# A convolution with three raw weight buffers, weight chunks mixed one ahead of their split, and the sums of the second sweep formed in place

## The reference, cut to what matters

```
x = lax.conv_general_dilated(inputs, conv_w, window_strides=(1,), padding='SAME',
                             dimension_numbers=('NWC', 'WIO', 'NWC')) + conv_b     # inputs (2, 2048, 1024), conv_w (3, 1024, 768)
q, k, v = jnp.split(x, 3, axis=-1)
# blocks of 128 tokens, 16 heads of 64: scores, causal softmax, values, two projections
x = _layernorm(x_in + attention_and_projections(q, k, v))
x = _layernorm(x + ffn(x))            # dense layer plus a mixture of low-rank experts
```

## Time and profile before

| | |
|---|---|
| time, median of 3 runs (lowest, highest) | 1656.67 us (1656.15, 1661.89) |
| time of the profiled execution | 1654.62 us |
| its span | 1652.8 us |
| PE busy in the span | 1566.8 us (95%) |
| DVE, ACT busy | 1183.8 us (72%), 610.5 us (37%) |
| matmuls of the convolution | 3456, from 14.4 to 463.1 us |
| first matmul after the convolution | 488.25 us |

### The profile page before, as it was taken

How to read it: one execution, slowest core, us unless ns; L and a number is a source line. 1 busy time by engine, 2 the same in 40 slices (tenths; PEclk the granted TensorE clock), 3 DMA queues, 4 the chain that set the end, 5 groups by cost and what they waited for, 6 DMA issues and landing times. The chain is left out here.

```text
span 1652.8 us, 29301 instructions
## 1 busy us (share of the span) xinstructions
PE 1566.8 (95%) x10816; PEld 1397.9 (85%) x10816; DVE 1183.8 (72%) x2785; ACT 610.5 (37%) x1729; POOL 260.7 (16%) x227
## 2 busy tenths in 40 slices
PE   6998999699938999999999999899999999999998
PEld 6998999699936888888888888689898988989897
DVE  6858857776656666666666667778878877887884
ACT  4223322322225776767667667611111111111110
POOL 0000000000001100101001010433333333333331
PEclk9999999899969999999999999999999999999999
DMA  7886564667850010110101021411121122112111
GB/s 291 329 277 259 211 214 164 210 232 270 292 195 6 2 52 1 51 51 0 51 0 51 28 80 54 143 62 58 62 81 57 57 74 69 57 67 76 57 42 51
DMA packets 55157, 181.05 MB, mean 110 GB/s; under 512 B 5552, under 2 KB 13872, under 8 KB 48432
## 3 DMA queue, kind: packets, MB, share of 16 engines
q1 hardware_dynamic: 53360, 173.81, 30.3%
q10 hardware_dynamic: 1728, 6.29, 1.0%
HBM read 125.49 MB, written 54.53 MB: 109 GB/s over the span
## 5 line engine op out<-in xcount | busy, mean ns | idle before, releaser
L588 PE MATMUL conv_acc<-x_split,weights 128*128 128x256 f32 x3456 | 423.6, 286 | 39.7 <-DVE weights L497 14.6
L588 PEld LDWEIGHTS conv_acc<-x_split,weights 128*128 128x128 f32 x3456 | 421.0, 194 | 42.2 <-issue 20.3
L1522 PE MATMUL ps_f<-weights 128*128 128x266 f32 (+2 forms) x1728 | 329.6, 344 | 0.0
L1522 PEld LDWEIGHTS ps_f<-weights 128*128 128x128 f32 x1728 | 277.5, 189 | 23.8
L1010 DVE CUSTOM_DVE_ANT_0 scores_and_probs<-ps_scores,causal_mask 128x128 f32<-128x128 f32 x512 | 118.6, 287 | 126.1 <-PE ps_scores L1130 122.2
L917 ACT ACTIVATE scores_and_probs<-scores_and_probs,score_neg_max 128x128 f32<-128x128 f32 x512 | 197.9, 392 | 4.8 <-DVE score_neg_max L1015 4.7
L1358 ACT ACTIVATE gate_exp<-h_and_gate,gate_neg_max 128x8 f32<-128x8 f32 x32 | 9.6, 301 | 349.6 <-DVE gate_neg_max L1433 349.6
L1101 PE MATMUL ps_v<-weights 128*128 128x512 f32 x384 | 106.2, 413 | 30.1 <-PEq L134 24.9
L355 ACT ACTIVATE x_split<-x_planes 128x1024 fp32r<-128x1024 f32 x48 | 51.0, 1062 | 210.7 <-PE conv_acc L588 166.6
L1522 PE MATMUL ps_f<-late_weights,weights 128*128 128x266 f32 (+2 forms) x576 | 116.1, 337 | 0.0
L475 DVE TENSOR_TENSOR x_split<-x_planes,x_split 128x1024 fp32r<-128x1024 f32 x48 | 58.7, 1223 | 75.3 <-ACT x_split L355 75.0
(11 more groups left out here) (136 smaller groups left out, 2355.8 us busy)
## 6 DMA issues: line engine op xcount, KB each, us to landing
x_raw<-in_xT SPq DMA_DIRECT2D x32, 1028.0 KB, 6.8
conv_tile<-in_x SPq DMA_DIRECT2D x32, 512.0 KB, 3.8
out<-out_tile SPq DMA_DIRECT2D x32, 512.0 KB, 2.7
conv_tile<-convT_scratch SPq DMA_DIRECT2D x16, 768.0 KB, 6.4
conv_tile<-in_conv_w SPq DMA_DIRECT2D x8, 1152.0 KB, 6.7
weight_stage<-in_conv_w SPq DMA_DIRECT2D x8, 1152.0 KB, 9.0
ce_scratch<-conv_l SPq DMA_DIRECT2D x16, 512.0 KB, 7.8
x_planes<-ce_scratch SPq DMA_DIRECT2D x16, 512.0 KB, 4.4
```

Of the source, the lines that this page charges most:

```text
L588: last = nc.tensor.matmul(acc[f][:, k, :], w[:, c, a, k, f * P:(f + 1) * P], xs[:, j % XS, b, k, c % CPG, :], start=(c == 0 and k == 0 and ...
L1522: mm = nc.tensor.matmul(ps_f[par][n][:, 0:b0 - a0], x1T[:, par, a, kc, :], wf[kc][:, b, a0:b0], start=(kc == 0 and k == 0), stop=(n == 2 a ...
```

## The change

Four things are done, all in `conv_phase`.

1. `conv_y` grows to the size of a raw weight chunk (128 x 2304) and becomes a third buffer for them: the load of chunk n now waits until chunk n - 3 is split, instead of n - 2. SP's loads of weights move: three before each boundary in single iterations, then in the iterations 17 to 20 and 32 to 34 those of chunks 3 and 4, 5 and 6, and 7, each right behind that iteration's load of inputs.
2. DVE mixes one chunk ahead of the split, and all of it stands at the end of the iteration: chunk 0 in iteration 14 (30), then in the iterations 15 to 18 (31 to 34) mix chunk c + 1, split chunk c, for two c. In the iterations from 31 on, the mix of the next inputs stands ahead of the weights, not behind.
3. Evacuation has three buffers, one for each pair p: the two of `conv_m` and `features_out`, which had been unused in the convolution. The first sweep, which had four, has these three as well.
4. `finish_first` writes sum and difference in place of its input, the second from the first, and SP stores from there. ACT therefore waits in the second sweep, and in the first unit of the third, until the stored piece (u - 1, p) has landed (`sd_stored`), no longer until DVE has read it.

The diff, cut to its core:

```diff
-    M_COUNT = 4
+    M_COUNT = FP
+    WR = 3
...
-        wraw = [craw[:, 0:TAPS * KTAPS].rearrange("p (k n) -> p k n", k=TAPS),
-                attn.stages[:, 0:TAPS * KTAPS].rearrange("p (k n) -> p k n", k=TAPS)]
...
-        ybuf = sb("conv_y", [P, 2 * QUAD * UQ], F32)
+        ybuf = sb("conv_y", [P, TAPS * KTAPS], F32)
+        wraw = [a.rearrange("p (k n) -> p k n", k=TAPS)
+                for a in (craw[:, 0:TAPS * KTAPS], attn.stages[:, 0:TAPS * KTAPS], ybuf[:])]
...
-        m = [pair_view(mbuf[:, i, :]) for i in range(2)]
-        y_half = [pair_view(ybuf[:, i * HALF:(i + 1) * HALF]) for i in range(2)]
-        m_first = m + y_half
-        sd = y_half
+        m = [pair_view(mbuf[:, i, :]) for i in range(2)] + [pair_view(attn.out[:].rearrange("p f n -> p (f n)"))]
...
             def load_w(n):
-                if n >= 2:
-                    sp.wait_ge(w_lo, n - 1)
+                if n >= WR:
+                    sp.wait_ge(w_lo, n - WR + 1)
...
-                sp.dma_start(sd_dram[n_of[u], p], sd[e % 2]).then_inc(sd_stored[e % 2], 16)
+                sp.dma_start(sd_dram[n_of[u], p], m[p]).then_inc(sd_stored[p], 16)
...
-                if j == 10:
-                    load_w(CC)
-                    load_w(CC + 1)
-                if 18 <= j < 18 + GRAN - 1:
-                    load_w(CC + CPG * (j - 17))
-                    load_w(CC + CPG * (j - 17) + 1)
-                if j == 26:
-                    load_w(2 * CC)
-                    load_w(2 * CC + 1)
+                if 10 <= j < 10 + WR:
+                    load_w(CC + j - 10)
+                if 17 <= j < 17 + GRAN:
+                    for n in range(CPG * (j - 17) + WR, min(CPG * (j - 16) + WR, CC)):
+                        load_w(CC + n)
+                if 24 <= j < 24 + WR:
+                    load_w(2 * CC + j - 24)
...
             for j in range(2 * GRAN * NU, J):
                 load_planes(j)
-                if j < 2 * GRAN * NU + 1 + GRAN - 1 and j > 2 * GRAN * NU:
-                    load_w(2 * CC + CPG * (j - 32))
-                    load_w(2 * CC + CPG * (j - 32) + 1)
+                if j < 2 * GRAN * NU + GRAN:
+                    for n in range(CPG * (j - 32) + WR, min(CPG * (j - 31) + WR, CC)):
+                        load_w(2 * CC + n)
                 for u, p in pieces(j - 2):
                     if u < 2 * NU:
                         store_sd(u, p)
...
-                    if s == 0:
-                        dst = m_first[e % M_COUNT]
-                        if e >= M_COUNT:
-                            act.wait_ge(m_stored[e % M_COUNT], 16 * (e // M_COUNT))
-                    else:
-                        dst, k = m[e % 2], e - ST_E
-                        if k < 2:
-                            act.wait_ge(m_stored[k], 16 * ST_E // M_COUNT)
-                        else:
-                            act.wait_ge(m_free, k - 1)
+                    dst = m[p]
+                    if 0 < u <= NU:
+                        act.wait_ge(m_stored[p], 16 * u)
+                    elif NU < u <= 2 * NU:
+                        act.wait_ge(sd_stored[p], 16 * (u - NU))
+                    elif u > 2 * NU:
+                        act.wait_ge(m_free, FP * (u - 2 * NU - 1) + p + 1)
...
-                nc.vector.tensor_tensor(dst[:, :, 0, :], a[:, :, 0, :], a[:, :, 1, :], ALU.add)
-                nc.vector.tensor_tensor(dst[:, :, 1, :], a[:, :, 0, :], a[:, :, 1, :], ALU.subtract).then_inc(m_free, 1)
-                dve.wait_ge(m_free, e + 1)
-                dve.sem_inc(fin_done, 1)
+                sums = step(nc.vector.tensor_tensor(a[:, :, 0, :], a[:, :, 0, :], a[:, :, 1, :], ALU.add), "f", fin_step)
+                dve.wait_ge(fin_step, sums)
+                stt(a[:, :, 1, :], a[:, :, 1, :], -2.0, a[:, :, 0, :]).then_inc(fin_done, 1)
...
+            def change_weights(j):
+
+                for s in range(1, SW):
+                    g = j - (GRAN * NU * s - 1)
+                    if g == -1:
+                        mix_weights(CC * s)
+                    if 0 <= g < GRAN:
+                        for c in range(CPG * g, CPG * g + CPG):
+                            if c + 1 < CC:
+                                mix_weights(CC * s + c + 1)
+                            split_weights(CC * s + c)
+
             mix(0)
             for j in range(J):
-                new = [CC * s + CPG * (j - GRAN * NU * s + 1) + i for s in range(1, SW)
-                       if 0 <= j - (GRAN * NU * s - 1) < GRAN for i in range(CPG)]
                 early = GRAN <= j < 2 * GRAN * NU - 1
                 if early:
                     mix(j + 1)
                 for u, p in pieces(j):
                     finish(u, p)
-                for n in new:
-                    mix_weights(n)
                 split_x(j)
...
                 if not early and j < J - 1:
                     mix(j + 1)
+                change_weights(j)
```

More of the change, by code:

```diff
@@ L178, in conv_phase @@
         bias_loaded = sem("conv_bias_loaded")
-        w_loaded = [sem(f"conv_w_loaded{i}") for i in range(2)]
+        w_loaded = [sem(f"conv_w_loaded{i}") for i in range(WR)]
         w_step, w_mix = sem("conv_w_summed"), sem("conv_w_mixed")
@@ L188, in conv_phase @@
         m_stored = [sem(f"conv_m_stored{i}") for i in range(M_COUNT)]
-        sd_stored = [sem(f"conv_sd_stored{i}") for i in range(2)]
+        sd_stored = [sem(f"conv_sd_stored{i}") for i in range(M_COUNT)]
         l_loaded = [sem(f"conv_l_loaded{i}") for i in range(2)]
@@ L204, in load_w @@
             def load_w(n):
-                if n >= 2:
-                    sp.wait_ge(w_lo, n - 1)
+                if n >= WR:
+                    sp.wait_ge(w_lo, n - WR + 1)
                 if n < CC:
-                    sp.dma_start(wraw[n % 2][:, 0:TAPS:2, :], conv_w[n % CC][:, 0:TAPS:2, :]).then_inc(w_loaded[n % 2], 16)
+                    sp.dma_start(wraw[n % WR][:, 0:TAPS:2, :],
+                                 conv_w[n % CC][:, 0:TAPS:2, :]).then_inc(w_loaded[n % WR], 16)
                 else:
-                    sp.dma_start(wraw[n % 2], conv_w[n % CC]).then_inc(w_loaded[n % 2], 16)
+                    sp.dma_start(wraw[n % WR], conv_w[n % CC]).then_inc(w_loaded[n % WR], 16)
             def store_ce(j):
@@ L233, in load_l @@
                     for i in range(M_COUNT):
-                        sp.wait_ge(m_stored[i], 16 * ST_E // M_COUNT)
+                        sp.wait_ge(m_stored[i], 16 * NU)
                 elif e == 1:
@@ L359, in split_weights @@
                 if s == 0:
-                    act.wait_ge(w_loaded[n % 2], 16 * (n // 2 + 1))
+                    act.wait_ge(w_loaded[n % WR], 16 * (n // WR + 1))
                 else:
@@ L363, in split_weights @@
                     act.wait_ge(x_used, GRAN * NU * s - GRAN + c // CPG + 1)
-                nc.scalar.activation(w[:, c, HI], wraw[n % 2][:, 0:TAPS:2, :], ACT.Copy).then_inc(w_hi, 1)
+                nc.scalar.activation(w[:, c, HI], wraw[n % WR][:, 0:TAPS:2, :], ACT.Copy).then_inc(w_hi, 1)
             def evacuate(u, pairs=range(FP)):
@@ L393, in evacuate @@
                         act.wait_ge(evac, e + 1)
-                        act.dma_start(m_dram[n_of[u], p], dst).then_inc(m_stored[e % M_COUNT], 16)
+                        act.dma_start(m_dram[n_of[u], p], dst).then_inc(m_stored[p], 16)
             def split_attn(n, after):
@@ L478, in mix_weights @@
             def mix_weights(n):
-                r = wraw[n % 2]
-                dve.wait_ge(w_loaded[n % 2], 16 * (n // 2 + 1))
+                r = wraw[n % WR]
+                dve.wait_ge(w_loaded[n % WR], 16 * (n // WR + 1))
                 if n < 2 * CC:
@@ L516, in finish_second @@
                 if e == 0:
-                    for i in range(2):
-                        dve.wait_ge(sd_stored[i], 16 * ST_E // 2)
+                    dve.wait_ge(w_lo, SW * CC)
                 elif e == 1:
@@ L532, in finish_second @@
                 y0 = step(nc.vector.tensor_tensor(y[0], y[2], s, ALU.add), "f", fin_step)
-                dve.wait_ge(m_free, ST_E + e + 1)
+                dve.wait_ge(m_free, e + 1)
                 y3 = step(stt(y[3], y[1], 8.0, d), "f", fin_step)
@@ L561, in _ @@
                     finish(u, p)
-                for n in new:
-                    mix_weights(n)
                 split_x(j)
                 if j < GRAN:
-                    new = list(range(CPG * j, CPG * j + CPG))
-                for n in new:
-                    split_weights(n)
+                    for n in range(CPG * j, CPG * j + CPG):
+                        split_weights(n)
                 if not early and j < J - 1:
                     mix(j + 1)
+                change_weights(j)
             split_attn(attn.WV)
```

15 lines of the change are left out of this document (5 added, 10 removed).

## The result

The change makes the kernel slower: 1663.6 us in the median of 20 runs (1662.0 to 1667.1) against 1656.8 us (1654.1 to 1662.6), a ratio of 1.004 with an interval of 1.0032 to 1.0047. That is 6.8 us, or 0.4%; the interval lies clear of no change. The profiled execution took 1663.0 us, with a span of 1661.2.

A forecast was written before the change was run, and what follows sets the result against it. PE, busy 95% of the span, was taken as the bound, with waits at two weight changes. Second boundary +14.5 and first -2.8 gave +11.7 on 1654.62, 1666.3; 2.05 from profile to median made 1668.4 us, range 1657 to 1675.

The forecast's parts named there:

- what had 0.28: The outcome same, neither under 1648.4 nor over 1665.0 us: A, C and the short end of the forecast, chance 0.28.
- Second boundary: PE's wait until 324.04: planes and stores land late behind weight loads, DVE and ACT wait, PE resumes 14.5 us later.
- both of my ends: Second boundary, landing of a store behind a weight load: 5.2 us as alone (+3.8), or 9.8 us (+21.8).
- First boundary: PE's wait until 168.03: ACT has chunk 5's high part 2.9 us earlier, a gain of 2.8 us.
- The start of the convolution: First sweep: the grown buffer and three evacuation buffers cost nothing, a buffer being needed again a unit (35 us) later.
- A: Second boundary: small transfers go round the weight load, landing as fast as alone; +1.0 us, 1657.7; with C 0.23.
- B: Second boundary works as the first, without waits: PE at 315.6, 8.4 us before 324.04, kernel faster, 1645.5; chance 0.07.
- C: Both boundaries: chunks no readier than before, one wait takes the place of another; 1656.7; with A 0.23.
- D: The chain is right and dearer: stores at 9.8 us, no first-boundary gain; +21.8, 1678.5; with the forecast 0.70.

The follow-up runs named there:

- the move in SP's list: The change with the weight loads of iterations 32 to 34 one iteration later in SP's list, behind the next planes and stores: 1642.9 us, ratio 0.9908.
- The last experiment: The kernel before with the third raw weight buffer in the first sweep alone: 1655.1 us against 1657.3 of before, ratio 0.9991 (0.9982 to 1.0001).
- the version without waits: The change with weight loads behind planes and stores in SP's list, and ACT emptying pair 2 before that iteration's two weight chunks: 1629.5 us, ratio 0.983.

## Why the prediction was right or wrong

The direction, the mechanism and its places were right; the size was 11.7 us for a measured 6.8 in the medians and 8.4 between the profiled executions. By the forecast's own line, slower was over 1665.0 us; at 1663.6 the change falls just short of it, in what had 0.28, although the interval lies clear of no change.

The forecast of 1668.4 is 4.8 us too high. About 1.1 of that is the second boundary, 0.6 the first, 0.6 the start of the convolution in the profiles, 1.1 what lies behind the start of the attention, and 1.5 the 2.05 us that I added to get from profile to median, where the change has 0.6.

- **Second boundary, +14.5; measured +12.8 to PE's resuming, +13.4 with its slower matmuls.** The chain ran as written, step by step. Taking off the 4.0 us by which DVE was earlier when it began (270.27 + 1.23 = 271.5 for 275.5), planes 33 were expected at 299.3 and mixed from 298.5; the store (6,1) at 317.8, and ACT began at 316.5; the store (6,2) at 333.1, ACT at 331.4; PE at 334.5, and it resumed at 332.9. Of the miss of 1.6 us, 1.3 are the weight loads ahead of the small transfers: 6.0, 6.2 and 6.3 us, where I had 6.6. A store behind it came after 6.9, 7.1 and 7.2 us, far from both of my ends (5.2 and 9.8), near the 7.4 of my sum. SP issued planes 33 at 290.8 (291.0 expected in this clock).
- **First boundary, -2.8; measured -3.4.** PE's wait fell by 3.75 us, of which 0.4 went into slower matmuls behind it. DVE came to the step 0.6 us sooner, as all of PE's clock did, and had chunk 5 mixed 0.9 us sooner than that, so the durations were a little too long. Nothing else was late, as expected.
- **The start of the convolution, costed at nothing.** This is the step that failed, and by this account the largest part of the miss, some 2 us. I said that the grown buffer costs nothing and did not ask what it gives in the first sweep, because the one profile of before shows a wait of 0.17 us there. That execution took 1654.6 us for a median of 1656.8; another waited 4.1 us. The last experiment puts some 2 us on it in the median, with an interval that reaches zero. It can explain why the profiles differ by 8.4 us and the medians by 6.8; that it does is likely, not shown.
- **The rivals.** A (small transfers go round a weight load) fell: in each trace they landed in order. Of the rule of the Trainium skill named there, "DMA: Bandwidth & Descriptors", section "Queues, rings and completion order", the landings agree with the first half, that descriptors are consumed in ring order; the second, that completion may be out of order, no run here shows at these sizes. B, the second boundary without waits, was priced at 8.4 us before 324.04; the move in SP's list made it real, and PE resumed at 309.7 in a kernel whose PE was 5.1 us ahead (267.01 for 272.13 at the start of unit 7), where B has 310.5: 1642.9 us for B's 1645.5. C fell, as PE's wait at the first boundary was 3.75 us shorter. D did not come: the stores took 7.2 us at most, not 9.8.
- **The price in the Trainium skill**, "DMA: Bandwidth & Descriptors", section "Anatomy of one DMA — SWDGE (gpsimd) path", is 2.0 us plus bytes over 436 GB/s, by which a weight load is estimated at 4.7 us. It is a fit to transfers issued from GpSimd; these are issued from SP, and they took 6.0 to 6.3 us. The sum by it, 1662.7 us, came nearer to the 1663.6 than mine, but by luck: a load priced too low made up for the parts of the miss named above that have nothing to do with loads.
- DVE's two waits for planes, ACT's two for stores and PE's three pieces of idle time were all there. PE's idle time at the second boundary was given as 26 to 30 us; it was 24.1.

## What to carry to other kernels

A load that waits for its buffer, written into an in-order issuing queue, is a barrier for everything behind it: write behind it only what is needed after the thing it waits for. Before adding a buffer, list for each small transfer behind a large one who waits for it first; here the same buffers and the same work gave +7 or -15 us by where five weight loads stood in a list. And one profile shows one execution: where each late landing puts off the next load, a wait of 0.2 us in it can be 4 us in the next.

## What was not expected of the hardware

Behind a load of 1152 KB, stores and loads of 512 KB on the same queue landed in order of issue, in the rows of before and in those of the change, 1.2 to 1.3 us apart, though alone they took 4.0 and 5.2 us: behind a large transfer a small one was cheap in itself and late all the same.

The granted clock of PE, from the answer by windows of the changed kernel (us, PE busy with matmuls, weight loads, DVE, ACT, POOL, PEclk, DMA share, GB/s):

```profile
310.00:320.00 10.00, 2.04 (x9) 2.04 (x10) 2.24 (x4) 2.76 (x5) 0.00 (x0) 0.50 0.65 218
320.00:330.00 10.00, 0.88 (x5) 0.59 (x3) 9.41 (x10) 1.48 (x1) 0.00 (x0) 0.50 0.49 152
330.00:340.00 10.00, 7.12 (x37) 7.13 (x37) 6.09 (x7) 4.46 (x7) 0.00 (x0) 0.55 0.52 174
340.00:350.00 10.00, 10.00 (x86) 10.00 (x85) 7.56 (x9) 1.80 (x2) 0.00 (x0) 1.00 0.65 220
```

In the two windows in which PE mostly stands still it is at 0.50, the lower level of 1.2 GHz, and at 1.00, 2.4 GHz, in the window after the one in which PE resumes. I had left this out of the sum. It cost little here, since before lost clock at each boundary too (0.75 from 160 to 170 us, 0.56 from 320 to 330): the 264 matmuls took 34.64 us for 34.05. Without any stop, 288 take 34.78, so 264 would take 31.9, an estimate; behind a stop they took 33.3 to 34.6 us in the profiles of both kernels, so a stop cost 1.4 to 2.8 us on top of its wait. That is part of why the version without waits gains more than the waits that it removes.
